# Expert tiles turned by VectorE in place, and gated z turned by way of a DRAM scratch

## What is computed

```
x = x + xattn(layernorm(x), ctx, ctx)
h = layernorm(x)                                   # per token
q = einsum('bsd,rd->bsr', h, Wq_w)                 # 16 router dimensions
scores = einsum('bsr,er->bse', q, keys)            # 64 experts
top_vals, top_idx = top_k(scores, 16)
gate = softmax of top_vals, put at the places of top_idx, else 0
z = einsum('bsd,nd->bsn', h, A_w)                  # 512 = 64 experts x 8
z_gated = z * gate (each gate value for 8 columns)
out = einsum('bsn,on->bso', z_gated, B_w) * 2
x = x + out
```

## Time and profile before

| | us |
|---|---|
| median of 3 runs | 2156.37 (2156.31 to 2156.42) |
| the profiled execution | 2156.57 |
| its span in the profile | 2154.8 |

### The profile page before, as it was taken

The page is one execution under the profiler, slowest core; times in us unless marked ns, Lnnn a source line. Parts: engine busy times, 40 slices in busy tenths (PEclk is TensorE's granted clock), DMA queues, the critical chain, the costliest instruction groups (busy, mean ns, idle before and its releaser), DMA issues.

```text
span 2154.8 us, 29239 instructions
## 1 busy us (share of the span) xinstructions
PE 2115.7 (98%) x8920; PEld 1328.0 (62%) x8920; DVE 1673.8 (78%) x4051; ACT 1337.5 (62%) x3051; POOL 1561.3 (72%) x965
## 2 busy tenths in 40 slices
PE   5999999999999999999999999999999999999999
PEld 2455455455455455454454454888888888888887
DVE  7999999999999999999999999644444444444443
ACT  4786786786786786786765646644444455445441
POOL 6999999999999999999999988633343433333420
PEclk9999999999999999999999999999999999999999
DMA  7232333333333332333221246544545444444431
GB/s 282 97 108 103 120 111 103 120 111 103 121 109 103 121 109 103 122 109 103 103 89 64 83 168 239 171 158 166 175 164 174 159 166 165 158 166 172 164 119 59
DMA packets 110705, 287.50 MB, mean 133 GB/s; under 512 B 7168, under 2 KB 7296, under 8 KB 109568
## 3 DMA queue, kind: packets, MB, share of 16 engines
q1 hardware_dynamic: 110592, 286.19, 38.3%
HBM read 219.06 MB, written 67.11 MB: 133 GB/s over the span
## 4 chain that ended last, share of the span: by engine, by line
PE 82%; DVE 7%; POOL 6%; ACT 2%; issue 2%; DMA 1%; SPq 0%; DVEq 0%; ACTq 0%; POOLq 0%
PE pair L755 11%; PE pair L749 8%; PE out L581 6%; PE out L582 6%; PE out L583 6%; PE z L583 5%; PE z L582 5%; PE z L581 5%; PE pair L644 5%; PE evac L631 4%; PE evac L655 4%; PE evac L656 4%; PE lag L698 4%; PE pair L745 4%; PE tp L600 2%; POOL r_f L1804 2%
## 5 line engine op out<-in xcount | busy, mean ns | idle before, releaser
L1838 POOL TENSOR_TENSOR rows<-rows,cin 128x1024 f32<-128x1024 f32 x48 | 117.0, 2437 | 325.7 <-DMA rows<-out_dram 273.6
L755 PE MATMUL pair<-r_f,back 128*128 128x512 f32 x768 | 342.7, 597 | 0.5 <-DVE prod L1035 0.5
L1804 POOL TENSOR_TENSOR r_f<-prod 128x1024 f32<-128x1024 f32 x128 | 303.0, 2378 | 9.3 <-DVE prod L1033 7.4
L755 PEld LDWEIGHTS pair<-r_f,back 128*128 128x128 f32 x768 | 143.0, 190 | 192.7 <-issue 146.5
L749 PE MATMUL pair<-w_sb,wts 128*128 128x512 f32 x512 | 225.1, 592 | 1.4 <-ACT w_sb L1625 0.9
L1480 ACT ACTIVATE xn<-tp 128x512 f32<-128x512 f32 x94 | 55.1, 586 | 231.0 <-PE tp L600 230.9
L581 PE MATMUL z<-a_hi,xt 128*128 128x512 f32 x496 | 195.9, 395 | 0.0
L581 PE MATMUL out<-b_hi,zt_hi 128*128 128x512 f32 x492 | 194.3, 395 | 0.0
L583 PE MATMUL z<-a_hi,xt 128*128 128x512 f32 x496 | 193.4, 390 | 0.0
L582 PE MATMUL z<-a_lo,xt 128*128 128x512 f32 x496 | 193.3, 390 | 0.0
L582 PE MATMUL out<-b_lo,zt_hi 128*128 128x512 f32 x492 | 191.6, 389 | 0.0
(11 more groups left out here) (234 smaller groups left out, 5576.8 us busy)
## 6 DMA issues: line engine op xcount, KB each, us to landing
out_dram<-att_sb SPq DMA_DIRECT2D x32, 1024.0 KB, 4.2
rows<-out_dram SPq DMA_DIRECT2D x64, 512.0 KB, 3.8
cin<-out_dram SPq DMA_DIRECT2D x63, 512.0 KB, 4.0
xin<-in_x_dram SPq DMA_DIRECT2D x63, 512.0 KB, 4.1
vf<-in_ctx_dram SPq DMA_DIRECT2D x31, 1024.0 KB, 5.1
out_dram<-rows SPq DMA_DIRECT2D x62, 512.0 KB, 2.8
xf<-in_x_dram SPq DMA_DIRECT2D x30, 1024.0 KB, 5.3
stat_in<-in_x_dram SPq DMA_DIRECT2D x27, 1024.0 KB, 5.1
```

The source lines that it names most:

```text
L755: return nc.tensor.matmul(pair_ps[:, bank, :], back[:, 3 * bank + n, :], r_f[:, row, :], start=n == 0, stop=n == 2)
L1804: nc.gpsimd.tensor_tensor(dst, prod[:, slot, 0:2, :], prod[:, slot, 2:4, :], ALU.add).then_inc(add_done, 1)
L1838: nc.gpsimd.tensor_tensor(half, first, other, op).then_inc(c_added, 1)
```

## The change

Tiles 4 to 31 and their gated z are no longer turned by TensorE. The product of a turned tile only needs some order of the 2048 features, if the weights have the same, and the change uses VectorE's transpose, which here turns 32 x 32 blocks where they lie. What must go to another group of 32 partitions is moved while the rows are normalized: ScalarE (`ACT_BLOCKS`) and VectorE (`DVE_BLOCKS`) each write eight pieces of 32 partitions x 512 columns of `xn`, each piece from one group of 32 rows into another group of partitions (`norm_blocks`). VectorE then transposes the four quarters of `xn` in place (`turn_spread`), ScalarE rounds them to the high half as before, and the low half now takes its first operand from `xn` in place of a PSUM bank. The weights are laid out on the host in the new order of features, and tiles 0 to 3 and the last z, which TensorE still turns, are written in that order (`norm_rows`, `gate_z`).

Gated z is stored from SBUF to a DRAM scratch `z_rows` by four DMAs of 512-byte pieces, loaded back in the moved order by one DMA, and transposed by VectorE into the PSUM bank `zt_ps`.

The order is changed too. SP stores z between the store of half 0 and the load behind it, and loads it behind the store of half 1. On VectorE the transposes and the statistics of half 0 come ahead of routing; low halves 3 and 4, the statistics of half 1 and the mean come ahead of output addition 1, and the gate behind it. TensorE's queries of tile u + 1 move between out banks 0 and 1 of step u.

```diff
@@ sync
+            def store_z(n):
+                sp.wait_ge(zg_ready, n)
+                rows_of = zg[:].rearrange("p (b f) -> p b f", b=4)
+                for c in range(4):
+                    sp.dma_start(z_rows.rearrange("(b j) (c f) -> c j b f", b=4, c=4)[c],
+                                 rows_of[SPREAD * c:SPREAD * (c + 1)]).then_inc(z_stored, 16)
+            def load_z(n):
+                sp.wait_ge(z_stored, 64 * (n - FIRST_SPREAD + 1))
+                sp.dma_start(zg[:], z_rows).then_inc(z_loaded, 16)
                     store_half(u, r, 0)
+                    if spread_z(u + 1):
+                        store_z(u + 1)
                     if later_tile(u + 1):
                         sp.wait_ge(out_stored, 16 * (2 * u - 1))
                         load_rows(k, 4 + r, 0)
                     store_half(u, r, 1)
+                    if spread_z(u + 1):
+                        load_z(u + 1)
@@ tensor
-                if b and not (is_step(u, 1) or is_step(u, TT)):
+                if b and not (is_step(u, 1) or is_step(u, TT) or spread_z(u)):
                     turn_z()
+                if spread_z(u):
+                    pe.wait_ge(zg_ready, u)
-                if f and not is_step(u, 0):
+                if f and not (is_step(u, 0) or spread(u + 1)):
                     for q in range(4):
                         turn_tile(u + 1, q)
...
                     for q in range(4):
+                        if q == 1 and f and not is_step(u, 1):
+                            for part in range(4):
+                                queries(u + 1, part)
                         out_bank(q)
@@ vector
-                nc.vector.tensor_tensor(xt[:, 1, part, :], tp_ps[bank_of(t, q)][:], xt[:, 0, part, :].bitcast(F32),
+                turned_x = xt_full[:, q, :, :] if spread(t) else tp_ps[bank_of(t, q)][:]
+                nc.vector.tensor_tensor(xt[:, 1, part, :], turned_x, xt[:, 0, part, :].bitcast(F32),
                                         ALU.subtract).then_inc(tp_lo, 1)
+            def turn_spread(t, q):
+                if q == 0:
+                    dve.wait_ge(xn_part, SPREAD_PARTS * (t - FIRST_SPREAD + 1))
+                part = xn[:, q * 512:(q + 1) * 512]
+                nc.vector.transpose(part, part).then_inc(tp_full, 1)
+            def norm_blocks(t, slot, blocks):
+                dve.wait_ge(norm2_ready, 2 * t + 2)
+                dve.wait_ge(q_ready, tp_at(t - 1, 3) + 1)
+                by_block = xn[:].rearrange("p (k c i) -> p k c i", k=KD, c=4)
+                for c in blocks:
+                    own = slice(SPREAD * c, SPREAD * (c + 1))
+                    for b in range(4):
+                        nc.vector.tensor_scalar(by_block[SPREAD * b:SPREAD * (b + 1), :, c, :],
+                                                rows[slot][own, b * 512:(b + 1) * 512].rearrange("p (k i) -> p k i", k=KD),
+                                                rstd2[own], shift2[own], ALU.mult, ALU.add).then_inc(xn_part, 1)
...
+                if spread_z(u):
+                    dve.wait_ge(z_loaded, 16 * (u - FIRST_SPREAD + 1))
+                    dve.wait_ge(zt_lo_done, u - 1)
...
+                    nc.vector.transpose(zt_ps[:].rearrange("p m (c j) -> p m c j", c=4),
+                                        zg[:].rearrange("p (c m i) -> p c m i", c=4, m=KN)).then_inc(zt_ready, 1)
                 if not is_step(u, TT):
                     zt_low()
+                if f and spread(u + 1):
+                    for q in range(4):
+                        turn_spread(u + 1, q)
+                if later_tile(u):
+                    half_statistics(u + 2, (r + 3) % RING, 0)
...
-                if later_tile(u):
-                    invert_root(u + 2)
+                if ahead(u):
+                    norm_blocks(u + 2, (r + 3) % RING, DVE_BLOCKS)
@@ scalar
+                if not spread(t):
+                    act.wait_ge(tp_ready, n + 1)
+                    nc.scalar.activation(xt_full[:, q, :, :], tp_ps[bank_of(t, q)][:], ACT.Copy).then_inc(tp_full, 1)
...
+                if f and not is_step(u, 1):
+                    copy_queries(u + 1)
+                if ahead(u):
+                    tile_scale(u + 2)
+                    norm_blocks(u + 2, (r + 3) % RING, ACT_BLOCKS)
```

More of the change, by code:

```diff
@@ L385, in turned_z, with spread, spread_z, ahead @@
             return xt[:, low, 0:KN, :] if is_step(u, TT) else (zt_lo if low else zt_hi)[:]
+        FIRST_SPREAD = 4
+        SPREAD = P // 4
+        SPREAD_PARTS = 16
+        ACT_BLOCKS, DVE_BLOCKS = (0, 1), (2, 3)
+        def spread(t):
+            return not (isinstance(t, int) and t < FIRST_SPREAD)
         def later_tile(u):
             return not (isinstance(u, int) and u + 2 >= TT)
+        def spread_z(n):
+            return not (isinstance(n, int) and (n < FIRST_SPREAD or n >= TT))
+        def ahead(u):
+            return later_tile(u) and spread(u + 2)
         def each_tile(eng, body):
@@ L835, in tile_step @@
                 elif a and not is_step(u, 1):
-                    for q in range(4):
-                        queries(u, q)
+                    if is_step(u, 2):
+                        for q in range(4):
+                            queries(u, q)
                     pe.wait_ge(tp_lo, tp_at(u, 3) + 1)
@@ L897, in tile_step @@
                 if b:
-                    if not f:
+                    if not f or spread(u + 1):
                         pe.wait_ge(zt_hi_done, u)
@@ L1379, in tile_step @@
                     tile_mean(u + 2)
+                add_out(1)
+                if later_tile(u):
+                    invert_root(u + 2)
+                if a:
+                    gate_z()
                 if is_step(u, TT - 1):
@@ L1508, in norm_rows, with norm_blocks @@
                 act.wait_ge(norm2_ready, 2 * t + 2)
-                nc.scalar.activation(xn[:], rows[slot][:], ACT.Identity, bias=shift2[:],
-                                     scale=rstd2[:]).then_inc(xn_ready, 1)
+                nc.scalar.activation(xn[:].rearrange("p (k b i) -> p b k i", b=4, k=KD),
+                                     rows[slot][:].rearrange("p (b k i) -> p b k i", b=4, k=KD),
+                                     ACT.Identity, bias=shift2[:], scale=rstd2[:]).then_inc(xn_ready, 1)
+            def norm_blocks(t, slot, blocks):
+                if blocks[0] == 0:
+                    act.wait_ge(norm2_ready, 2 * t + 2)
+                    act.wait_ge(tp_lo, tp_at(t - 1, 3) + 1)
+                by_block = xn[:].rearrange("p (k c i) -> p k c i", k=KD, c=4)
+                for c in blocks:
+                    own = slice(SPREAD * c, SPREAD * (c + 1))
+                    for b in range(4):
+                        nc.scalar.activation(by_block[SPREAD * b:SPREAD * (b + 1), :, c, :],
+                                             rows[slot][own, b * 512:(b + 1) * 512].rearrange("p (k i) -> p k i", k=KD),
+                                             ACT.Identity, bias=shift2[own], scale=rstd2[own]).then_inc(xn_part, 1)
             act.wait_ge(consts_set, 2)
@@ L1747, in tile_step @@
                 else:
-                    if f:
-                        norm_tile(u + 1, (r + 2) % RING)
+                    if is_step(u, 2):
+                        norm_tile(3, 3)
                     zt_high()
                 if f:
+                    act.wait_ge(z_ready, u + 1)
                     for q in range(4):
-                        if q == 0:
-                            act.wait_ge(z_ready, u + 1)
-                        if q == 2:
+                        if is_step(u, 1) and q == 2:
                             exponentials()
                         tile_high(u + 1, q)
-                elif a:
+                if a and not is_step(u, 1):
                     exponentials()
```

43 lines of the change are left out of this document (24 added, 19 removed).

## The result

| kernel | median us (runs) | ratio to before, 95% interval | profiled execution, its span |
|---|---|---|---|
| before | 2156.37 (2156.31 to 2156.42) | | 2156.57, 2154.8 |
| after | 2180.93 (2177.58 to 2183.0) | 1.0112 [1.0092, 1.0132] | 2177.58, 2175.4 |

What follows compares the result with a forecast made beforehand. The prediction took a load-to-load loop of 25.0 us as the bound, against steps of 25.33: 7.9 us from 24 steps, plus 3.1, 1.7, 2.2 and 0.5, less 2.4, gain 13.0 from 2156.57, forecast 2143.5 us, range 2104 to 2180.

Steps and rivals of the forecast that it cites:

- the loop: From one load of half 0 through GpSimd's additions, VectorE and z stores to the next load: 25.0 us a step.
- The turns: VectorE's low halves, both inputs in SBUF, alternate with GpSimd's 2.4 us additions; low halves last 0.69 to 3.1 us.
- the first rival: TensorE stays the bound, since low halves need not take turns with GpSimd: 2098 us; chance 0.20 for 2098 to 2125.
- The ends: Step 30 gains 2.2 us and step 31 0.5; gate and z of the last tile come later, losing 2.4.
- Load to addition: Load of half 0 issued to its partner addition on GpSimd: 4.08 us, plus 0.3 for z data queued ahead.
- Stores of z: Four z stores on SP at 0.36 us each and a notice of 0.1, ahead of the load: 1.5 us.
- Half 0 to half 1: GpSimd's partner addition of half 0 to that of half 1: 7.25 us, the mean of 6.90 and 7.60.
- the second rival: The loop is longer than the old step: 26.35 us, about 2176; chance 0.17 for 25.4 to 26.4 us.
- Low halves and output addition 0: On VectorE, two low halves waiting for GpSimd's additions, then output addition 0 and low halves 3 and 4: 7.85 us.
- the third rival: VectorE's eight blocks collide with GpSimd's additions from about 0.5 us a block: loop some 26.3 us, 2180; chance 0.16.
- The blocks: VectorE's eight normalizations of 32x512 a step: 0.45 us each, through before GpSimd's addition of half 0 if up to 0.43.
- Z by way of DRAM: Gated z's load lands 6 to 7 us into the step, not late; out starts at 11.2 us.

Runs made afterwards that it cites:

- experiment 1: The changed kernel, but low halves of tiles 4 to 31 take their first operand from an idle PSUM bank (output wrong): 2114.25 us.
- kernel 8: Experiment 7's kernel with ScalarE writing 12 of the 16 pieces and VectorE four: 2102.13 us, 0.9746 of before.
- experiment 6: The changed kernel with all tiles turned by TensorE again; gated z still goes through the DRAM scratch: 2150.29 us, 0.9967 of before.
- experiment 4: The changed kernel with SP issuing the load of the next rows' half 0 ahead of the z stores: 2159.97 us, 1.0014 of before.
- experiment 2: The changed kernel, but VectorE's eight blocks read an idle PSUM bank in place of the rows (output wrong): 2174.51 us.
- experiment 9: The changed kernel with one edit, ScalarE writing 12 of the 16 pieces and VectorE four: 2174.11 us, 1.0077 of before.
- experiment 5: The changed kernel with gated z turned by TensorE again, without scratch; tiles still turned by VectorE: 2141.18 us, 0.9935 of before.
- experiment 7: The changed kernel with VectorE turning tiles into PSUM, ScalarE copying them back, low halves reading PSUM, rows loaded before z stores: 2144.17 us.
- experiment 10: The changed kernel with all 16 pieces written to the partitions they are read from (output wrong): 2176.38 us, 1.0086 of before.

## Why the prediction was wrong

The mechanism was right, and its size was not: the forecast had a loop of 25.0 us against a step of 25.33, a margin of 0.33 us, and the loop came out at 26.2. What held:

- **The turns.** Low halves of up to 2.89 us, as forecast (0.69 to 3.1), and experiment 1 shows that without them the kernel is at 2114, where the first rival had 2098.
- **The idle time of TensorE.** Forecast were 1.8 us a step at out banks 2 and 3. The view of the waits has 41.4 us in 600 us, or 22.9 steps, which is 1.8.
- **What leaves TensorE.** 2.17 us a step were forecast, and kernel 8 shows 2.04. The four transposes of z are worth 0.34 us (experiment 6), not 0.5.
- **The ends.** The last two steps gained 2.8 (forecast 2.7), the tail lost 2.3 (2.4).

What failed, by the terms of the sum:

- **Load to addition, 4.08 + 0.3 for the data of z in front.** It is 5.04 in the mean. With the 256 KB of z in front that is 1.0 us more than 4.08, not 0.3; with the load ahead of them (experiment 4) it is 4.23. The range had 1.3 as its other end: the true value lay near it. The data in front may not be all of it: in the five steps in which the blocks collide, the store of half 1 is issued 0.5 us later behind the load, and the addition comes 4.1 to 4.5 us after the load with the same z in front.
- **Stores of z, 1.5.** Four issues took 1.82 us of SP, 0.45 each in place of the 0.36 read from a store that stands alone, and 2.0 with the notices: 0.5 us more.
- **Half 0 to half 1, 7.25.** 7.59, and the second rival had taken 7.60. The row 7.60 stood beside 6.90 in the earlier trace rows and the mean of two was taken. 0.35 us.
- **Low halves and output addition 0.** Forecast from the partner addition to the statistics 2.40 + 0.65 + 2.40 + 2.40 = 7.85; in the step above 7.44. This term was 0.4 too long. Statistics and mean (1.81), addition 1 (0.67) and gate (1.51) came out as read.

The misses sum to 0.66 + 0.5 + 0.35 - 0.4 = 1.1 us of the 1.2 between 25.0 and 26.2. Over the whole run: at the scores of tile 6 after is 2.0 us behind before (1497.1 against 1495.1), where the steps before the loop builds up were to have gained 4.8, which is 7 us; the 23 steps from there to tile 29 take 601.9 us, where 23 of 25.0 take 575, which is 27 us. Together that is the 34 us between the forecast and the profiled execution (2177.6). The result is by its loop the second rival, "the loop is longer than the old step", whose price of 26.35 us fits within 0.2 us a step. Its time of 2176 is 5 us short; 2181 lies in the band of the third rival, 2170 to 2190, which priced nearly the same loop (26.3) at 2180, without the 5 us that the steps outside the loop were to gain. It was given 0.17, because both of its terms were taken from the middle and the end was called a range.

**The blocks.** 0.45 us was taken, 0.543 measured (0.57 from start to start), beyond the 0.5 from which the third rival was to decide. They did collide, in six groups of 28, and cost little: at most 0.25 us a step (experiment 2), and 0.13 by the steps of experiment 9. Why not more: the load of the rows was itself late, so that the addition of half 0 mostly started 4.6 to 5.2 us after the first block, when the blocks (4.57) were through. Where it is not late (experiments 4, 5 and 7) they collide in nearly every step. The two rivals thus exclude each other in part; the prediction had priced them as if each came by itself. The Trainium skill, page "VectorE: DVE Perf Modes", section "The perf-mode tier table", puts this operation at twice the rate of a two-source one, and its subsection "Why PSUM operands drop a tier" an fp32 PSUM source back at the single rate. The order is confirmed here, with 0.543 us from SBUF, 0.68 for a two-source one (the low half) and 0.814 from PSUM, though not the factor of two; the estimate of 0.42 us made from it was too low.

**ScalarE's pieces.** 0.55 us was taken, 0.814 measured. In after nothing waits for them. The row to read was in the trace of before: the wide normalization L1509, 128 x 2048 with the same two scalars, takes 2101 ns, and the 128x512 copy L1480, without them, 582 ns; I had taken the price of the copy. The Trainium skill, page "ScalarE: Activation LUTs", section "What ACT_TABLE_LOAD costs", gives each such scalar about 93 ns on top of 186 ns and 0.833 ns per element; that makes an estimated 0.80 us for 512 columns with two of them, and experiment 10 agrees (0.801).

**Z by way of DRAM.** Forecast was that its load lands 6 to 7 us into the step and is not late. It lands later, as in this step:

```profile
1877.17 4.56 DVE L1055 TENSOR_SCALAR xn<-rows,rstd,shift 32x512 f32<-32x512 f32 x8
...
1884.41 0.73 DVE L1432 STREAM_TRANSPOSE zt<-zg 128x512 f32<-128x512 f32 x1 [2.67 <-DMA zg<-z_rows]
```

The z matmuls of this step start at 1876.25 and the load of z is issued at 1878.00, behind both stores. VectorE waits 2.67 us for it and turns z 8.2 us into the step (7.7 in the median of all steps, never past 8.6 where it waits for the load, so under the 9 that the prediction named); in the median the load takes 5.6 us, for half the bytes of a load of rows. Low half and transposes end some 12.8 us in, where the forecast had 11.4, and then come the statistics of half 0 (1.2 us), which stand ahead of the scores in the new order and which the forecast had left out. So routing starts 13.8 us in (1890.07), not 11.3. The low halves still meet GpSimd's additions, since these are as late. Thus two chains run into the low halves, that of the rows by way of GpSimd and that of z by way of VectorE. The trace of after shows which one holds. In 21 of the 28 steps the first two low halves meet both additions of half 1. VectorE gets to them 0.9 to 2.2 us after the partner addition has started, as z came early or late, and yet the statistics of half 1 always start 7.43 to 7.46 us after that addition. So in these steps the lateness of z cost nothing, and the rows by way of GpSimd set the pace, as the prediction had it. In the six steps behind a collision VectorE gets there 4.3 to 5.0 us after the start of the partner addition, and is the late one itself. (The page's chain runs through the load of z for 4% of the span, but there the waiting for GpSimd's additions stands as "issue", since no semaphore tells of it.)

## What to carry to other kernels

Before work is moved to an idle engine, look at which memory its operands come from: an operand that moves from PSUM to SBUF can tie two engines together that had nothing to do with each other, and here that one operand was worth 67 us of 2181. When a gain rests on a cyclic chain that is only a few tenths of a microsecond shorter than the present step, add up the upper ends of its terms as well, and let the chance of a loss follow from how many of them need to be true. And when two collisions share a resource, removing one moves the other: the same split of the blocks was worth 7 us alone and 42 us once the low halves were out of the way.

## What the runs showed that was not expected

- **TensorE's clock fell behind some short waits, and in those steps the blocks collide.** In the step above out bank 2 waited 1.84 us for output addition 0. The stretches before, during and after that wait, with the granted clock in the third column from the right:

```profile
1890.00:1894.00 4.00, 3.89 (x45) 2.98 (x44) 3.84 (x14) 2.90 (x5) 3.92 (x2) 1.00 0.11 37
1894.00:1896.20 2.20, 0.44 (x2) 0.01 (x1) 2.20 (x3) 0.00 (x0) 1.07 (x1) 1.00 0.58 196
1896.30:1899.90 3.60, 3.60 (x9) 2.88 (x10) 3.51 (x13) 0.37 (x2) 0.00 (x0) 0.55 0.41 139
1900.00:1903.40 3.40, 3.40 (x16) 2.84 (x15) 1.77 (x4) 3.21 (x7) 0.00 (x0) 0.99 0.57 203
```

  The clock goes from 1.00 (2.4 GHz) to 0.55, nearly all of that stretch at 1.2 GHz, and back. Nine matmuls stand in 3.6 us where 16 fit in 3.4 at full clock, which costs some 1.6 us of TensorE. It happens five times between 1500 and 2060 us, each time at out bank 2 behind a wait of 1.8 to 2.0 us, and not behind five other waits there of 1.8 to 2.4 us. Here are the stretches behind the longest of those five and behind one of 1.82 us:

```profile
1477.60:1481.10 3.50, 3.01 (x12) 2.17 (x12) 3.41 (x12) 0.37 (x2) 0.00 (x0) 1.00 0.41 147
1582.20:1585.80 3.60, 3.60 (x9) 2.80 (x10) 3.51 (x13) 0.37 (x2) 0.00 (x0) 0.56 0.43 140
```

  These five steps are the five of 28.6 to 29.0 us. Out banks 2 and 3 end later, so the last output addition and the blocks behind it start 1.0 us after the load of half 0 and not 0.0 to 0.35, and the addition of half 0 comes 3.1 to 3.5 us after the first block, when they aren't through. That the clock brings the collision about rests on this order in time and on five cases of five; no run holds the clock up. In the kernel of experiment 10 four of seven such stretches are followed by a collision, and in that of experiment 1 one group collides with none before it. What decides behind which wait the clock falls is open, and so is what the lost clock alone costs in time.
- **VectorE's transpose of fp32.** 128x512 in place takes 0.670 us, from start to start 0.60; into a PSUM bank 0.684, and for z 0.727. The forecast of 0.60 was right.
- **GpSimd and VectorE alternate.** GpSimd's two additions stand one behind the other, and yet a block of VectorE gets in between. The last two blocks of the step above, from the chain of after: start, duration.

```profile
1907.81 2.65 DVE xn L1055
1910.49 2.51 DVE xn L1055
```

  The first waits for the partner addition (from 1907.78), the second for the input addition (from 1910.25), and neither for both.
